# Two routing stages dissolved into the steps of the attention stages beside them

## The reference

```python
xn = _layernorm(x, axis=-1)
x = x + _L1_attn_ref(xn, ...) + _L1_ffn_ref(xn, ...)
xn = _layernorm(x, axis=-1)
x = x + _L2_attn_ref(xn, ...) + _L2_ffn_ref(xn, ...)
# both _ffn_ref: scores of the experts, the best two, their weighted sum
scores = softmax(xf @ w_router.T, axis=-1)
expert_weights, expert_indices = jax.lax.top_k(scores, 2)
out = jnp.sum(expert_weights[:, :, None] * expert_output_of(expert_indices), axis=1)
```

## Time and profile before

| | |
|---|---|
| median of 3 executions | 1866.82 us (1863.52 to 1869.09) |
| the profiled execution, its own time | 1876.44 us |
| its span | 1874.6 us |
| TensorE busy | 1572.7 us (84%) |
| VectorE busy | 1178.6 us (63%) |
| ScalarE busy | 1005.7 us (54%) |
| GpSimd busy | 368.8 us (20%) |
| granted TensorE clock, mean | 0.919 of full speed |
| layer 1: gate stage, from its first work to the attention's | 763.43 to 783.36 us |
| layer 2: gate stage, from its first work to the attention's | 1171.73 to 1190.81 us |

### The profile page before, as it was taken

The page is one execution under the profiler, slowest core; times in us unless marked ns, Lnnn a source line. Parts: engine busy times, 40 slices in busy tenths (PEclk is TensorE's granted clock), DMA queues, the critical chain, the costliest instruction groups (busy, mean ns, idle before and its releaser), DMA issues. The chain is left out here.

```text
span 1874.6 us, 32014 instructions
## 1 busy us (share of the span) xinstructions
PE 1572.7 (84%) x10886; PEld 1096.7 (58%) x10886; DVE 1178.6 (63%) x3074; ACT 1005.7 (54%) x2696; POOL 368.8 (20%) x381
## 2 busy tenths in 40 slices
PE   3799999759999998599999894588889665999855
PEld 2577777536666666377777763455557523555533
DVE  5599997557777776554545345666633375877754
ACT  2488887516666666254544342144344247999721
POOL 0100000000000000111111052543304302888700
PEclk9899999969999999599999997799999877999966
DMA  4000000030000000300000022200101211222200
GB/s 134 1 1 1 1 1 1 24 111 1 1 1 1 1 1 1 112 10 8 10 8 25 1 76 79 99 15 13 30 10 59 72 30 41 86 89 84 65 0 23
DMA packets 43789, 62.50 MB, mean 33 GB/s; under 512 B 7384, under 2 KB 29728, under 8 KB 42816
## 3 DMA queue, kind: packets, MB, share of 16 engines
q1 hardware_dynamic: 39088, 51.08, 9.0%
q0 software_dynamic: 4544, 9.38, 1.4%
HBM read 49.88 MB, written 15.75 MB: 35 GB/s over the span
## 5 line engine op out<-in xcount | busy, mean ns | idle before, releaser
L561 ACT ACTIVATE probs<-psum_all,pair_negmax 128x256 f32<-128x256 f32 x512 | 235.8, 473 | 160.3 <-DVE pair_negmax L660 88.5
L1986 POOL TENSOR_TENSOR weighted<-state,c_all 128x512 f32<-128x512 f32 x128 | 160.3, 1275 | 95.1 <-DVE state L1996 67.4
L1996 DVE TENSOR_TENSOR_SCAN state<-decay,psum_all 128x512 f32<-128x512 f32 x128 | 148.9, 1206 | 43.5 <-PE psum_all L1915 43.5
L660 DVE TENSOR_REDUCE pair_negmax<-psum_all 128x2 f32<-128x512 f32 x192 | 123.7, 686 | 66.8 <-PE psum_all L476 66.8
L686 DVE TENSOR_SCALAR probs<-probs,pair_recip 128x256 f32<-128x256 f32 x512 | 146.1, 349 | 4.5
L476 PE MATMUL psum_all<-keys,queryT 64*128 64x256 f32 x1024 | 144.1, 400 | 2.5 <-ACT probs L561 2.5
L572 ACT ACTIVATE probsT<-psum_all 128x512 f32<-128x512 f32 x256 | 140.0, 611 | 0.7 <-PE psum_all L487 0.5
L501 PE MATMUL psum_all<-probsT,values 128*64 128x256 f32 x1024 | 138.8, 392 | 0.0
L487 PE MATMUL psum_all<-ident,probs 128*128 128x128 f32 x1024 | 133.1, 273 | 2.8 <-ACT probsT L572 1.8
L487 PEld LDWEIGHTS psum_all<-ident,probs 128*128 128x128 f32 x1024 | 119.1, 141 | 18.1 <-issue 4.4
L476 PEld LDWEIGHTS psum_all<-keys,queryT 64*128 64x128 f32 x1024 | 92.6, 189 | 54.4 <-issue 46.4
(11 more groups left out here) (357 smaller groups left out, 3169.8 us busy)
## 6 DMA issues: line engine op xcount, KB each, us to landing
c_all<-c_rows SPq DMA_DIRECT2D x64, 256.0 KB, 3.2
slots<-slot_fill_dram SPq DMA_DIRECT2D x2, 2535.0 KB, 14.1
ring<-slots SPq DMA_DIRECT2D x18, 260.0 KB, 2.8
keys<-found SPq DMA_DIRECT2D x16, 256.0 KB, 4.7
up<-up_dram SPq DMA_DIRECT2D x1, 2048.0 KB
down<-down_dram SPq DMA_DIRECT2D x1, 2048.0 KB
up<-up_dram SPq DMA_DIRECT2D x1, 1408.0 KB
found<-values,dest POOLq DMA_INDIRECT x78, 2.2
```

The source lines that it names most:

```text
L561: nc.scalar.activation(k.probs[:, 2 * (u % PAIR_BUF) + j, t, :], k.psum[score_bank(u, j)][:, SEQ * t:SEQ * (t + 1)], ACT.Exp, bias=k.pair_ ...
L660: nc.vector.reduce_max(k.pair_negmax[:, u % 2, SUB * j:SUB * (j + 1)], src, AXX, negate=True).then_inc(s.negmax_ready, 1)
L1986: nc.gpsimd.tensor_tensor(w.weighted[:, u % RING, :], w.state[:, u % RING, :], w.c_all[:, u // L3_DC % C_RING, :], ALU.mult)\
L1996: nc.vector.tensor_tensor_scan(w.state[:, u % RING, :], w.decay[:, u % L3_RING, :, :].rearrange("p b n -> p (b n)"), k.psum[u % PARTS_RING ...
```

## The change

`gate_stage` is gone, and with it both of its calls. Its work becomes part of the attention stages of the same layer:

- The logits are two jobs of 8 tiles each, behind the other jobs of steps 0 and 1, and the counts are one job behind those of step 8 (`COUNT_AT`). VectorE saves each from PSUM to SBUF, and the rest of the work reads these copies.
- VectorE's part is cut into pieces, each behind the jobs of a step (`gate_at_step`): centring in step 2, share 4, comparisons 5, ranks and marks 6, best expert 7, weights 8, counts 9, tiles 10, places 11, slots 12, and in layer 2 the division by the sum in 13. ScalarE's exponential comes behind step 3.
- GpSimd, not ScalarE, copies `xn` into `rows`: in layer 1 ahead of the scatters, in layer 2 behind the keys of m = 4. It also clears `padded_values` at the start of layer 2's attention.
- The scatters wait for the slots. In layer 1 two go behind the scores of each of the steps 11 to 26. In layer 2 GpSimd sends three for each m from 8 on, the second and third each behind the scores of another step, and the last eight one by one behind the turned scores 24 to 31.
- Each attention stage has six semaphores more (`gate_step`, `centred`, `exped`, `marked`, `slots_found`, `rows_copied`); the gate stage had seven.

```diff
+COUNT_AT = 8
...
+def gate_centre(nc, k, w, dve, s, step):
+    step.add(nc.vector.memset(k.gate_cmp[:, :, :, :], 0.0))
+    step.add(nc.vector.tensor_copy(w.rows[:, :, P], gate_consts(k)[5]))
+    step.add(nc.vector.reduce_max(k.gate_sum[:, :], k.gate[:, :, :], AXX))
+    step.wait()
+    nc.vector.tensor_tensor(k.gate[:, :, :], k.gate[:, :, :], k.gate_sum[:, :].unsqueeze(2).to_broadcast([P, TILES, L1_E]), ALU.subtract)\
+        .then_inc(s.centred, 1)
...
+def gate_compare(nc, k, w, dve, s, step, experts):
+    E = L1_E
+    step.wait()
+    for j in experts:
+        rival = k.gate[:, :, j:j + 1]
+        if j > 0:
+            step.add(nc.vector.tensor_tensor(k.gate_cmp[:, j, :, 0:j], rival.to_broadcast([P, TILES, j]), k.gate[:, :, 0:j], ALU.is_gt))
+        if j < E - 1:
+            step.add(nc.vector.tensor_tensor(k.gate_cmp[:, j, :, j + 1:E], rival.to_broadcast([P, TILES, E - 1 - j]), k.gate[:, :, j + 1:E], ALU.is_ge))
+def gate_mark(nc, k, w, dve, s, step):
+    step.wait()
+    step.add(nc.vector.reduce_sum(k.gate_rank[:, :, :].rearrange("p t e -> p (t e)"), k.gate_cmp[:, :, :, :].rearrange("p j t e -> p (t e) j"), AXX))
+    step.wait()
+    nc.vector.tensor_scalar(k.gate_mask[:, :, :].rearrange("p e t -> p t e"), k.gate_rank[:, :, :], 2.0, None, ALU.is_lt).then_inc(s.marked, 1)
...
+    totals = k.count_parts[:, E * TILES:2 * E * TILES]
+    step.add(nc.vector.tensor_tensor_scan(k.counts[:, :, :].rearrange("p e t -> p (e t)"), carry, totals, 0.0, ALU.mult, ALU.add))
...
+def slot_finish(nc, k, w, dve, s, step):
+    step.wait()
+    for r in range(2):
+        step.add(nc.vector.scalar_tensor_tensor(k.gate_pick[:, r, :, :], k.gate_rank[:, :, :], float(r), k.gate[:, :, :], ALU.is_equal, ALU.mult))
+    step.wait()
+    step.add(nc.vector.reduce_sum(k.slot_float[:, :, :], k.gate_pick[:, 0:2, :, :], AXX))
+    step.wait()
+    nc.vector.tensor_scalar(k.slot[:, :, :], k.slot_float[:, :, :], -1.0, float(SLOTS - 1), ALU.add, ALU.min).then_inc(s.slots_found, 1)
+def gate_at_step(nc, k, w, dve, s, step, g, renormalise):
+    if g == 2:
+        gate_centre(nc, k, w, dve, s, step)
+    if g == 4:
+        gate_share(nc, k, w, dve, s, step)
+    if g == 5:
+        gate_compare(nc, k, w, dve, s, step, range(L1_E))
+    if g == 6:
+        gate_mark(nc, k, w, dve, s, step)
+    if g == 7:
+        gate_top_expert(nc, k, w, dve, s, step)
+    if g == 8:
+        gate_pick(nc, k, w, dve, s, step)
+    if g == COUNT_AT + 1:
+        slot_counts(nc, k, w, dve, s, step)
+    if g == COUNT_AT + 2:
+        slot_tiles(nc, k, w, dve, s, step)
+    if g == COUNT_AT + 3:
+        slot_places(nc, k, w, dve, s, step)
+    if g == COUNT_AT + 4:
+        slot_finish(nc, k, w, dve, s, step)
+    if g == COUNT_AT + 5 and renormalise:
+        gate_renormalise(nc, k, w, dve, s, step)
...
+    late[0].append(("logits", 0, 0))
+    late[1].append(("logits", 0, 1))
+    late[COUNT_AT].append(("counts", 0, 0))
...
+    SEND_FROM = 8
...
                 nc.gpsimd.memset(k.row_max[:, :, :, :, :], 0.0).then_inc(s.ones_set, 1)
+                nc.gpsimd.memset(w.padded_values[:, :, :, :, :], 0.0).then_inc(s.ones_set, 1)
+                pool.wait_ge(s.ones_set, 2)
                 nc.gpsimd.memset(w.padded_values[:, :, :, :, L2_D:L2_D + 1], 1.0).then_inc(s.ones_set, 1)
...
-                    for t in range(2):
-                        send_rows(nc, k, w, s, 2 * m + t)
+                    if m == 4:
+                        nc.gpsimd.tensor_copy(w.rows[:, :, 0:P], k.xn[:, :, :]).then_inc(s.rows_copied, 1)
+                    if m == SEND_FROM:
+                        pool.wait_ge(s.slots_found, 1)
+                        pool.wait_ge(s.rows_copied, 1)
+                    if m >= SEND_FROM:
+                        for t in range(3):
+                            if t >= 1:
+                                pool.wait_ge(s.scores_ready, 2 * m - 2 + t)
+                            send_rows(nc, k, w, s, 3 * (m - SEND_FROM) + t)
+                sent = 3 * (2 * BATCH - SEND_FROM)
+                for t in range(sent, 2 * TILES):
+                    pool.wait_ge(s.turned_ready, N - 2 * TILES + t + 1)
+                    send_rows(nc, k, w, s, t)
...
+                    if what == "logits":
+                        for t in range(8):
+                            at = P * (8 * i + t)
+                            last = nc.tensor.matmul(jb[:, L1_E * t:L1_E * (t + 1)], k.xnT[:, at:at + P], w.router[:, :], start=True, stop=True)
+                    elif what == "counts":
+                        pe.wait_ge(s.marked, 1)
+                        mask = k.gate_mask[:, :, :].rearrange("p e t -> p (e t)")
+                        for j in range(2):
+                            last = nc.tensor.matmul(jb[:, P * j:P * (j + 1)], k.counting[:, P * j:P * (j + 1)], mask, start=True, stop=True)
+                    elif what in ("straight", "swapped"):
...
+                    if g == 3:
+                        act.wait_ge(s.centred, 1)
+                        nc.scalar.activation(k.gate[:, :, :], k.gate[:, :, :], ACT.Exp).then_inc(s.exped, 1)
...
+                    if what == "logits":
+                        ins = nc.vector.tensor_copy(k.gate[:, 8 * i:8 * (i + 1), :].rearrange("p t e -> p (t e)"), jb[:, 0:8 * L1_E])
+                    elif what == "counts":
+                        ins = nc.vector.tensor_copy(k.count_parts[:, :], jb[:, 0:2 * P])
...
+                    if g == 2:
+                        wait_saved(dve, ("logits", 0, 1))
+                    if g == COUNT_AT + 1:
+                        wait_saved(dve, ("counts", 0, 0))
+                    gate_at_step(nc, k, w, dve, s, gating, g, True)
...
+    slots[2][0].append(("logits", 0, 0))
+    slots[2][1].append(("logits", 0, 1))
+    slots[2][COUNT_AT].append(("counts", 0, 0))
...
+                pool.wait_ge(s.background, 5)
+                nc.gpsimd.tensor_copy(w.rows[:, :, 0:P], k.xn[:, :, :]).then_inc(s.rows_copied, 1)
+                pool.wait_ge(s.slots_found, 1)
+                pool.wait_ge(s.rows_copied, 1)
                 for t in range(2 * TILES):
-                    if t >= 4:
-                        pool.wait_ge(s.scores_ready, t - 3)
+                    pool.wait_ge(s.scores_ready, COUNT_AT + 4 + t // 2)
                     send_rows(nc, k, w, s, t)
...
-def gate_stage(nc, k, w, router, renormalise, zeros=()):
...
-        gate_stage(nc, k, w, w.router[:, :], False)
...
-        gate_stage(nc, k, w, w.router[:, :], True, zeros=(w.padded_values[:, :, :, :, :],))
```

More of the change, by code:

```diff
@@ new lines, in gate_pick, with gate_renormalise @@
+def gate_pick(nc, k, w, dve, s, step):
+    for r in range(2):
+        step.add(nc.vector.scalar_tensor_tensor(k.gate_pick[:, r, :, :], k.gate_rank[:, :, :], float(r), k.gate[:, :, :], ALU.is_equal, ALU.mult))
+    step.wait()
+    step.add(nc.vector.reduce_sum(k.gate_top[:, :, :], k.gate_pick[:, 0:2, :, :], AXX))
+def gate_renormalise(nc, k, w, dve, s, step):
+    step.wait()
+    step.add(nc.vector.tensor_tensor(k.gate_sum[:, :], k.gate_top[:, 0, :], k.gate_top[:, 1, :], ALU.add))
+    step.wait()
+    step.add(nc.vector.reciprocal(k.gate_sum[:, :], k.gate_sum[:, :]))
+    step.wait()
+    step.add(nc.vector.tensor_tensor(k.gate_top[:, :, :], k.gate_top[:, :, :], k.gate_sum[:, :].unsqueeze(1).to_broadcast([P, 2, TILES]), ALU.mult))
@@ new lines, in slot_counts @@
+def slot_counts(nc, k, w, dve, s, step):
+    E = L1_E
+    limits, carry = gate_consts(k)[2:4]
+    totals = k.count_parts[:, E * TILES:2 * E * TILES]
+    step.add(nc.vector.tensor_tensor_scan(k.counts[:, :, :].rearrange("p e t -> p (e t)"), carry, totals, 0.0, ALU.mult, ALU.add))
+    step.wait()
+    step.add(nc.vector.tensor_tensor(k.above[:, :, :], k.counts[:, :, TILES - 1:TILES].to_broadcast([P, E, TILES]),
+                                     limits.unsqueeze(1).to_broadcast([P, E, TILES]), ALU.is_gt))
+    step.wait()
+    step.add(nc.vector.reduce_sum(k.taken[:, 0, :], k.above[:, :, :], AXX))
+    step.add(nc.vector.tensor_tensor(k.counts[:, :, :], k.counts[:, :, :], totals.rearrange("p (e t) -> p e t", e=E), ALU.subtract))
@@ new lines, in slot_tiles @@
+def slot_tiles(nc, k, w, dve, s, step):
+    E = L1_E
+    consts = gate_consts(k)
+    step.wait()
+    step.add(nc.vector.tensor_tensor_scan(k.taken[:, 1, :], consts[1], k.taken[:, 0, :], 0.0, ALU.mult, ALU.add))
+    step.wait()
+    step.add(nc.vector.tensor_tensor(k.taken[:, 0, :], k.taken[:, 1, :], k.taken[:, 0, :], ALU.subtract))
+    step.add(nc.vector.tensor_tensor(k.past[:, :, :], k.taken[:, 1, :].unsqueeze(1).to_broadcast([P, SLOT_TILES, E]),
+                                     consts[4].unsqueeze(2).to_broadcast([P, SLOT_TILES, E]), ALU.is_le))
+    step.wait()
+    step.add(nc.vector.scalar_tensor_tensor(k.counts[:, :, :], k.taken[:, 0, :].unsqueeze(2).to_broadcast([P, E, TILES]), float(P),
+                                            k.counts[:, :, :], ALU.mult, ALU.add))
```

(33 more changed lines are left out.)

132 lines of the change are left out of this document (25 added, 107 removed).

## The result

The changed kernel took 1852.9 us, the median of four executions (1851.5 to 1853.6), against 1867.6 for the kernel before on the same chip: a ratio of 0.9924, 95% interval 0.9909 to 0.994. That is 14.7 us less; forecast were 17.9 less and 1848.9 us. The profiled execution took 1851.5 us, its span 1849.5.

A forecast was written before the change was run, and what follows sets the result against it. No engine saturated overall; TensorE bounds layer 1's attention, a ring of waits layer 2's. Layer 1 -14.3, layer 2 -4.5, semaphores +0.9 gave -17.9 us: 1866.8 to 1848.9, range 1839 to 1858.

The forecast's parts named there:

- Removed: Both gate stages, 19.93 us in layer 1 and 19.08 in layer 2, vanish: -39.0 us.
- Layer 1, TensorE: Layer 1's attention: two logits jobs 3.8 us, wait 0.3, count job 0.6 plus 0.7: +5.4, range 3.5 to 8.6.
- Layer 1, VectorE: Layer 1's attention: VectorE's pieces fit its 3.2 us hole, costing only 0.2 us; low end 0, high end 8.
- The rival of unhidden pieces: Layer 1: normalising, squaring and products pass through the delayed VectorE; +8 us, so 1857; chance 0.13.
- Layer 2, first steps: Layer 2's attention before step 4: logits waits 3.15 twice, centring 1.65, less 1.0 coming back: +7.1 us.
- The 1.0 that should come back with the scatters: Layer 2, scores of step 4: GpSimd's keys no longer late behind four scatters and an addition; -1.0 us.
- Layer 2, steps 4 to 13: Each VectorE piece costs what exceeds the 0.8 us hole, step 8 1.1: together +5.0 us, range 3 to 13.
- The term for GpSimd beside VectorE: Layer 2, step 5: comparisons wait out GpSimd's key sums alone, +2.5 us; bounds 0 and 7.0.
- the 7.0 worked out from all of GpSimd's work: Layer 2, step 5: comparisons wait out sums 2.5 and copy 4.5; as a rival +4.5 more, 1853 us, chance 0.17.
- Scatters and tail: Scatters fit their steps in both layers and slot loads land in time: 0; late-scatter rival +3 us, 1852, chance 0.05.
- Semaphores: Ends of the two attention stages: six semaphores more each, 0.07 us apiece, 12 cost +0.9 us.
- the rival of 0.03: TensorE held at half clock three to four steps more loses the gain; at six, 1882 us or so; chance 0.03.

The follow-up runs named there:

- logits_wide: Layer 1's router padded with zeros from 8 to 64 columns, against the changed kernel: 1867.93 us, beside 1865.77 for the changed kernel.
- logits_ob: Layer 2's two logits jobs write to a free bank, against the changed kernel: 1859.54 us, 6.2 less, ratio 0.992.
- the second reading: Profile of the kernel before with only layer 1's scatters timed anew, eight of them back to back; 1868.16 us, 1.0004 of the kernel before.
- act_copy: Layer 2's copy of the normalised rows done by ScalarE at the stage's start, not GpSimd, against the changed kernel: 1864.62 us, medians differ by 1.2.
- compare6: Changed kernel with layer 2's comparisons and ranks one step later (steps 6 and 7): 1860.56 us, 0.994 of the kernel before.

## Why the prediction was nearly right

- **Removed**: 19.9 and 19.3 us, as forecast.
- **Layer 1, TensorE**: passes 1.92 and 1.90, wait 0.47 (0.3 forecast), counts 1.41 (1.3): 5.7 for 5.4. But steps 0 to 31 grew by 8.1 to 8.4. The rest is half clock behind the jobs, 1.0 us in one pair of passes, some 2.5 in all: the forecast had half clock for the logits only as its high end, and nothing for the passes behind them. `logits_wide` shows for the second job that it comes with the 8 columns; for the first it is open.
- **Layer 1, VectorE**: right. Apart from steps 0 to 2 and 8, all steps to 31 are those of the kernel before to 0.02 us. The idle time before the normalisation shrank in five steps between 3 and 13, at most from 3.87 to 1.70 us (step 7), and never to none. The rival of unhidden pieces is out.
- **Layer 2, first steps**: steps 0, 1 and 2 grew by 3.5, 3.8 and 0.9, 8.2 for 8.1. `logits_ob` shows that most of the 7.3 was the wait with the clock behind it. The 1.0 that should come back with the scatters was not seen: step 3 took 6.18 us, 6.12 before. Instead the stage's first scores came 1.4 us earlier, as its first 16 passes ran at full clock (3.69 us, 5.14 before). So from the stage's start to step 4 it is +6.6 to +6.9, forecast +7.1, and this is luck: the two later traces of the same kernel began at half clock (5.19 and 5.66 us) and have +10 and +12.
- **Layer 2, steps 4 to 13**: +9.0 by the second reading (+10.8 by the first), forecast 5.0 + 2.5. The term for GpSimd beside VectorE measured 3.2 and not 2.5 (5.1 - 1.9): 1.7 the copy, which was put at nothing, and 1.5 the sums, put at 2.5 (`act_copy`, `compare6`). The rule of the Trainium skill, "SBUF — State Buffer", section "Who interferes with whom", that a VectorE instruction with two SBUF inputs waits for GpSimd's reads, is borne out by 1.87 us beside the copy. Yet the 7.0 worked out from all of GpSimd's work was far too much, for two reasons: that work took 4.8 us, since the copy was 2.01 and not the 4.5 of the addition, and only one comparison waited out each of the long instructions, the others slipped between. Another 1.9 us is half clock behind the 4.67 us in which TensorE stood: 4.2 us for two groups of passes that take 2.3. The pieces themselves took some 3.9 for 5.0.
- **Scatters and tail**: 0 in layer 2, right: steps 13 to 31 differ by 0.1 us, and the loads were in time. In layer 1 they were costed at nothing, and that held in the first trace only; in the seven others with that order of scatters step 14 cost 3.6 us or more. **Semaphores**: 1.78 and 1.81 us for 1.47, +0.3 a stage, 0.6 for 0.9.

So the failed step is the clock. The forecast weighed it in whole steps, as the rival of 0.03, and put at nothing the short stretches of half clock behind narrow jobs and long waits; they cost some 2.5 us in layer 1 and 1.9 in layer 2. With the 0.7 of GpSimd beside VectorE and some 1.7 by which other terms were too high, that makes the 3.4 us between 17.9 and 14.5.

That the measured time fell so near the forecast owes something to where it was taken. On two other chips the same kernel gained only 9.3 and 7.4 us, half of what was forecast or less. Beside the first trace, the traces from there are 3.7 us longer in step 14, and 3.5 and 5.5 us longer from the start of layer 2's attention to step 4. The forecast has no term for either. What stays open is the stall: what "remote" stands for was not found, nor why ScalarE is late too, nor why the kernel before is free of it.

## What to carry to other kernels

When a stage is dissolved into its neighbour, price each piece by what stands behind it: a job that shares a bank with the one before costs its wait as well as its passes, and a free bank saved 6 us here. Look for GpSimd's work beside every run of short VectorE instructions with two SBUF operands; one step later they took 1.9 us in place of 5.1. Look at the clock behind each new wait of TensorE and each job of narrow passes: here it cost one to two microseconds at a time. Profile more than one execution, if possible on more than one chip, before a term under 5 us is believed.

## What the runs showed of the hardware

- The granted clock fell to half behind 16 passes of 8 columns (1.90 us) during which TensorE was busy all the time (0.58 from 792 to 796 us), and did not behind 16 passes of 64 columns (1.95 us, granted 1.00): step 2 took 8.92 us in all eight traces with 8 columns and 7.43 in both with 64.
- A VectorE comparison of two SBUF operands took 1.87 us beside GpSimd's copy of 2.01 us, and 0.18 without it; of 14 in a row only single ones waited, 5.1 us for all in place of 1.9, beside 4.8 us of GpSimd's work.
- With the new layer 1 and eight scatters in a row, VectorE's addition in step 14 started 2.1 to 2.3 us after its operand was ready, without a releaser in the profile, in seven traces of eight, and ScalarE's squaring before it 0.7 to 1.5 us late in the same seven.
- One execution differs from another in the same steps by more than some edits: layer 2's first four steps took 22.9, 25.0 and 26.7 us in three traces of one kernel, and steps 13 to 31, which the change leaves as they are, 99.0 us in two traces and 101.2 to 103.7 in twelve.
